# Low halves of the second feed-forward weights: from VectorE to TensorE and ScalarE, in a reordered opening

## The reference

```python
h = relu(layernorm(x))                       # block 0, a graph attention
Wh = h @ W;  e = leaky(Wh@a1 [:,None] + Wh@a2 [None,:])   # slope 0.2
att = softmax(where(adj > 0, e, -inf))
att = where(att < 16th largest of its row, 0, att)
x = x + elu(att @ Wh)
y = relu(layernorm(x))                       # block 1, three layers
for l in range(3):
    s = leaky(y@w_i[l] [:,None] + y@w_j[l] [None,:] + b[l])
    agg = softmax(where(adj + eye > 0, s, -inf)) @ y
    z = layernorm(y + agg) * g1[l] + beta1[l]
    ff = gelu(z @ W1[l] + b1[l]) @ W2[l] + b2[l]   # 256 -> 1024 -> 256
    y = layernorm(z + ff) * g2[l] + beta2[l]
out = x + y
```

## Time and profile before

| | us |
|---|---|
| median of 3 runs | 2819.51 (2818.25 to 2822.01) |
| the profiled execution | 2820.53 |
| its span in the profile | 2818.1 |
| PE busy in the span | 2712.6 (96%) |
| ACT busy | 2328.5 (83%) |
| DVE busy | 2302.2 (82%) |
| POOL busy | 2082.3 (74%) |

### The profile page before, as it was taken

One profiled execution on the slowest core, in us unless ns is written; L12 is line 12 of the kernel. 1 busy time (PEld: TensorE's weight loads), 2 busy tenths in 40 slices (PEclk: granted clock), 3 DMA queues, 4 the chain that ended last, 5 costly groups with the idle time before them and its releaser, 6 DMA issues.

```text
span 2818.1 us, 55394 instructions
## 1 busy us (share of the span) xinstructions
PE 2712.6 (96%) x17764; PEld 2441.1 (87%) x17764; DVE 2302.2 (82%) x7766; ACT 2328.5 (83%) x4808; POOL 2082.3 (74%) x2217
## 2 busy tenths in 40 slices
PE   5799999999999999999999999999999999999995
PEld 4688888889899999889999899999989998888884
DVE  6889878888888888888888888888888888887542
ACT  3788898888888888888888888888888888888763
POOL 1466777787777778877778777777877777877774
PEclk9899999999999999999999999999999999999997
DMA  5110110101110110110110111011111011010001
GB/s 167 47 29 22 36 31 28 35 9 35 34 35 27 35 25 19 35 35 28 35 35 9 35 35 35 27 35 22 22 35 35 28 36 33 14 22 20 11 10 15
DMA packets 96323, 88.64 MB, mean 31 GB/s; under 512 B 9120, under 2 KB 94368, under 8 KB 96032
## 3 DMA queue, kind: packets, MB, share of 16 engines
q1 hardware_dynamic: 79136, 68.32, 7.9%
q0 software_dynamic: 16896, 16.78, 4.6%
HBM read 47.34 MB, written 37.75 MB: 30 GB/s over the span
## 4 chain that ended last, share of the span: by engine, by line
PE 72%; POOL 9%; issue 7%; ACT 6%; DVE 4%; DMA 2%; SPq 0%; POOLq 0%; ACTq 0%; DVEq 0%
PE ps_ff L3065 10%; PE ps_mm L3042 10%; PE ps_mm L3044 9%; PE ps_ff L3066 9%; PE ps_ff L3067 9%; PE ps_mm L3043 9%; PE ps_ag L3100 5%; PE ps_ht L3112 2%; POOL a_lo L506 2%; PE ps L3164 2%; DMA out<-H 2%; POOL H L496 1%; PE ps_s L3088 1%; POOL H L513 1%; ACT X L1083 1%
## 5 line engine op out<-in xcount | busy, mean ns | idle before, releaser
L3065 PE MATMUL ps_ff<-w_hi,a_hi 128*128 128x256 f32 x3072 | 892.9, 291 | 12.6 <-POOL a_lo L506 5.9
L506 POOL TENSOR_TENSOR a_lo<-A,a_hi 128x512 fp32r<-128x512 f32 x384 | 527.3, 1373 | 482.6 <-ACT a_hi L1077 482.3
L3066 PE MATMUL ps_ff<-w_lo,a_hi 128*128 128x256 f32 x3072 | 855.2, 278 | 0.0
L3067 PE MATMUL ps_ff<-w_hi,a_lo 128*128 128x256 f32 x3072 | 854.6, 278 | 0.0
L1069 ACT ACTIVATE A<-ps_mm,b_col 128x512 f32<-128x512 f32 x768 | 517.3, 685 | 250.3 <-PE ps_ff L3067 140.7
L3042 PE MATMUL ps_mm<-ht_hi,w_hi 128*128 128x512 f32 x1536 | 625.7, 407 | 6.7 <-DVE ht_lo L2327 4.3
L3065 PEld LDWEIGHTS ps_ff<-w_hi,a_hi 128*128 128x128 f32 x3072 | 577.9, 188 | 50.6 <-issue 13.3
L3044 PE MATMUL ps_mm<-ht_lo,w_hi 128*128 128x512 f32 x1536 | 605.5, 394 | 0.0
L3043 PE MATMUL ps_mm<-ht_hi,w_lo 128*128 128x512 f32 x1536 | 603.6, 393 | 0.0
L3066 PEld LDWEIGHTS ps_ff<-w_lo,a_hi 128*128 128x128 f32 x3072 | 579.0, 188 | 12.1
L3067 PEld LDWEIGHTS ps_ff<-w_hi,a_lo 128*128 128x128 f32 x3072 | 579.0, 188 | 0.0
(11 more groups left out here) (120 smaller groups left out, 5320.8 us busy)
## 6 DMA issues: line engine op xcount, KB each, us to landing
xr<-in_x SPq DMA_DIRECT2D x32, 512.0 KB, 4.0
out<-x SPq DMA_DIRECT2D x32, 512.0 KB, 4.8
out<-H POOLq DMA_DIRECT2D x32, 512.0 KB, 6.1
mask_in<-mask_park SPq DMA_DIRECT2D x96, 128.0 KB, 4.0
adj_sb<-in_adj SPq DMA_DIRECT2D x32, 256.0 KB, 4.4
mask_park<-mask_out SPq DMA_DIRECT2D x32, 128.0 KB, 3.9
X<-in_L_gnn_W SPq DMA_DIRECT2D x3, 1024.0 KB, 5.2
H<-in_L_gnn_W SPq DMA_DIRECT2D x3, 1024.0 KB, 8.6
```

What stands on the lines that cost most here:

```text
L506: pool.tensor_tensor(a_lo[:, at], A[:, at], a_hi[:, at].bitcast(F32), ALU.subtract).then_inc(s["a_lo_gpsimd"], 1)
L3065: pe.matmul(out_g, a_hi[:, at, cols], w2_hi[:, l, m], start=first, stop=False, skip_group_check=True)
L3066: pe.matmul(out_g, a_hi[:, at, cols], w2_lo[:, l, m], start=False, stop=False, skip_group_check=True)
L3067: last = pe.matmul(out_g, a_lo[:, at, cols], w2_hi[:, l, m], start=False, stop=final, skip_group_check=True)
```

## The change

The low halves of W2 are made by other engines. PE writes the F32 staging values through the identity into a bank, and subtracts the high half through a negated identity; ScalarE copies the bank out as F32R. Each layer is cut into four quarters q of 512 columns. The negated identity lies in a part of ht_hi that is free until unit (1,0). The banks are ps_ag and ps_ht for layer 0, ps_s and ps_ag for layers 1 and 2, so waits come with it that keep these apart from scores and agg.

```diff
+        neg_ident = ht_hi[:, 0, 0, 0:P]
+        def w2_bank(l, q):
+            return (ps_ag, ps_ht)[q % 2] if l == 0 else (ps_s, ps_ag)[q % 2]
...
             def load_w2(l):
-                    sp.wait_ge(s["w2_split"], l)
+                    sp.wait_ge(s["w2_split"], 4 * l)
...
             def ht_high(k, l, d):
+                if peeled(k, 1) and l == 0:
+                    act.wait_ge(s["w2_diffed"], 4 * L)
...
+            def neg_ident_copy():
+                act.wait_ge(s["const_made"], 4)
+                act.activation(neg_ident, ident[:], ACT.Copy, scale=-1.0).then_inc(s["neg_made"], 1)
+
+            def w2_low(l, q):
+                act.wait_ge(s["w2_diffed"], 4 * l + q + 1)
+                act.activation(w2_flat[2][l][:, q * 512:(q + 1) * 512], w2_bank(l, q)[:], ACT.Copy).then_inc(s["w2_split"], 1)
...
-            def w2_low(l):
-                dve.wait_ge(s["w2_hi_made"], l + 1)
-                tt(w2_lo[:, l], w2_stage, w2_hi[:, l].bitcast(F32), ALU.subtract).then_inc(s["w2_split"], 1)
...
             def mm2(k, l, m):
-                        pe.wait_ge(s["w2_split"], l + 1)
+                        pe.wait_ge(s["w2_split"], 4 * l + 4)
             def turn_sj(k, l):
+                if peeled(k, 1) and l == 0:
+                    pe.wait_ge(s["w2_split"], 4 * L)
             def agg(k, l, half):
+                if peeled(k, 0) and l == 0 and half == 0:
+                    pe.wait_ge(s["w2_split"], 4)
...
+            def w2_diff(l, q):
+                c, cols = 4 * l + q, slice(q * 512, (q + 1) * 512)
+                pe.wait_ge(s["w2_hi_made"], l + 1)
+                if c == 0:
+                    pe.wait_ge(s["neg_made"], 1)
+                if c > 1:
+                    pe.wait_ge(s["w2_split"], c - 1)
+                if c == 4:
+                    pe.wait_ge(s["pt_made"], 1)
+                if c == 5:
+                    pe.wait_ge(s["y1_made"], 2)
+                pe.matmul(w2_bank(l, q)[:], ident[:], w2_flat[0][:, cols], start=True, stop=False)
+                last = pe.matmul(w2_bank(l, q)[:], neg_ident, w2_flat[1][l][:, cols], start=False, stop=True)
+                last.then_inc(s["w2_diffed"], 1)
```

More of the change, by code:

```diff
@@ L1228, in opening @@
                 mix_high(1, 0)
-                w2_high(1)
+                w2_low(1, 0)
+                w2_low(1, 1)
                 h_norm(0, 0)
+                elu_exp(1, 0)
+                mix_high(1, 1)
                 ht_high(0, 0, 0)
-                mix_high(1, 1)
-                elu_exp(1, 0)
+                w2_low(1, 2)
+                w2_low(1, 3)
+                w1_high(2)
                 ht_high(0, 0, 1)
@@ L1463, in opening @@
+                h_norm(4, 0)
                 mix_high(5, 0)
-                a_high(1, 2, 3)
                 gelu(1, 2, 4)
-                h_norm(4, 0)
-                leaky(3, 1)
+                a_high(1, 2, 4)
                 ht_high(4, 0, 0)
-                a_high(1, 2, 4)
-                y_norm(2, 1)
                 gelu(1, 2, 5)
+                a_high(1, 2, 5)
                 gelu(1, 2, 6)
-                a_high(1, 2, 5)
-                exps(3, 1)
-                elu_exp(5, 0)
+                gelu(1, 2, 7)
@@ L1476, in opening @@
                 a_high(1, 2, 6)
                 ht_high(4, 0, 1)
-                p_copy(3, 1)
-                mix_high(5, 1)
-                gelu(1, 2, 7)
-                gelu(4, 0, 0)
-                a_high(1, 2, 7)
-                elu_exp(5, 1)
-                a_high(4, 0, 0)
-                gelu(4, 0, 1)
+                a_high(1, 2, 7)
+                y_norm(2, 1)
+                mix_high(5, 1)
+                leaky(3, 1)
+                gelu(4, 0, 0)
+                elu_exp(5, 0)
@@ L1497, in opening @@
-                leaky(2, 2)
-                ht_high(3, 1, 0)
-                gelu(4, 0, 6)
-                a_high(4, 0, 6)
-                gelu(4, 0, 7)
-                ht_high(3, 1, 1)
-                a_high(4, 0, 7)
-                r_norm(5)
+                a_high(4, 0, 3)
+                elu_exp(5, 1)
+                gelu(4, 0, 4)
+                gelu(4, 0, 5)
+                a_high(4, 0, 4)
+                h_norm(3, 1)
+                gelu(4, 0, 6)
+                a_high(4, 0, 5)
@@ L3196, in opening @@
                 agg(0, 0, 0)
+                w2_diff(1, 0)
+                agg(0, 0, 1)
                 turn_z(1)
-                agg(0, 0, 1)
                 z_mix(1, 0)
+                w2_diff(1, 1)
+                z_agg(1, 0)
+                w2_diff(1, 2)
+                z_mix(1, 1)
+                w2_diff(1, 3)
+                turn_h(0, 0, 0)
                 w1_bias(2)
-                z_agg(1, 0)
-                turn_h(0, 0, 0)
-                z_mix(1, 1)
                 turn_h(0, 0, 1)
@@ L3215, in opening @@
                 mm1(0, 0, 6)
+                w2_diff(2, 0)
+                w2_diff(2, 1)
+                mm1(0, 0, 7)
                 mm2(0, 0, 3)
-                mm1(0, 0, 7)
+                w2_diff(2, 2)
+                w2_diff(2, 3)
                 mm2(0, 0, 4)
+                turn_sj(1, 0)
                 mm2(0, 0, 5)
```

1016 lines of the change are left out of this document (515 added, 501 removed).

## The result

The changed kernel takes 2829.31 us, the median of 6 runs (2828.93 to 2831.16); the kernel before took 2820.29 beside it. The ratio is 1.0031, with a 95% interval of 1.0021 to 1.0041: 9 us slower, where 3 us faster was forecast, and outside the range. The profiled execution has a span of 2827.1 us against 2818.1.

The account below looks back on a forecast made before the run. TensorE, busy 96%, was taken to bound the kernel after a serial opening chain; -1.3 us to mm1(0,0,0), -1.7 to mm1(1,0,0) and 0 after gave -3.0 us, a median of 2816.5, 8 in 10 within 2810.5 to 2823.5.

Parts of the forecast that it names:

- (J): Everything after mm1(1,0,0): no change, 0, with bounds of -7.6 and +3 us.
- (A): Start of the kernel: load_a0 second in SP's queue shortens VectorE's wait of 2.59 us; -1.0 us.
- (B): Layer 0 differences in TensorE's waits around z_mix and z_agg; +0.8, 0 and +0.9 us at the upper clock.
- (C): In group 0's attention, z_out(0,1) no longer waits behind other VectorE work that now comes later; -2.8 us.
- (D): Differences fill TensorE's waits, so the clock rises from about 31 us and z_agg and z_mix shorten; -3.6 us.
- Rival 1: Slower: TensorE stays at the lower clock until mm1(0,0,0); +7.4 us, 2826.9 us, chance 0.10.
- (E): From r_moments(0) to node_scores(0,0), VectorE's work there of 7.1 us exceeds the 6.2 us latency; +0.9 us.
- (G): w2_diff(1,0) between the two halves of agg, in a wait of 1.1 us; +0.6 us.
- (H): From agg(0,0,1) to mm1(0,0,0), three more differences and w1_bias(2) moved later; +2.9 us, bounds +2.0 and +6.3.
- (I): Unit (0,0) and the way to mm1(1,0,0), ScalarE's list setting the pace; -1.7 us, bounds -4 and +1.5.
- Rival 3: Clearly faster: the new opening order also saves about half the 7.6 us idle after 160 us; -8.1 us, chance 0.25.
- Rival 2: No change: unit (0,0) pays +1.5 us as differences push mm1 and mm2 back; total +0.2 us, chance 0.17.

Follow-up runs that it names:

- the first seam: Changed kernel up to mm1(1,0,0), about 135 us, on every engine, then the order of the kernel before; 2815.65 us, 0.9981 of the kernel before.
- the seam at 272: Changed kernel's queues up to mm1(0,2,6), at 272 us, then the order of the kernel before; its total time is not given in the text.
- the seam at 345: Changed kernel's queues up to mm1(1,2,3), at 345 us, then the order of the kernel before; as slow as the changed kernel.
- the two kernels with moved steps: Changed kernel with add_out(1) behind a_low(3,1,6) on GpSimd, 2829.37 us (1.0029); the same plus ht_low(3,1,1) ahead of y_sum(4,0) on VectorE, 2830.93 us (1.0034).

## Why the prediction was wrong

The step that failed is **(J)**, everything after mm1(1,0,0): 0, with bounds of -7.6 and +3. It measured +9.5 us to the end of the span: +12.4 by the end of the opening, and some -3 in the closing, which no step of the prediction had. I took the idle time of before as what there was to gain, and an order that waits "somewhat more" as all there was to lose, though the five queues were rewritten up to 500 us, and no row of before can bound what a different order waits. The new order without the differences loses 12.9 us there, the differences in the old order nothing; and the kernel with the seam at 135, which has the changed kernel up to mm1(1,0,0) and the old order behind it, is 0.19% faster than before. That it is 5.7 us faster and not 0.5 is no merit of the forecast: most of it arises outside the opening.

The other steps:

- **(A)** -1.0: DVE starts on the row sums at 8.38 in place of 9.27, -0.9. Right. W0 now lands last, its bound.
- **(B)** A difference takes 2.24 us at the lower level (28.27 to 30.51) and 1.09 at the upper (34.40 to 35.49), against 2.3 and 1.15; the twelve copies take 0.58 to 0.60 each by their groups in the trace. Right. With **(C)** and **(D)**, z_out(0,1) starts 6.1 us earlier, forecast -5.7. The clock rises at 31 us, as forecast, and the two orders, each with and without the differences, show that these bring it. Rival 1 is refuted.
- **(E)** +0.9: from r_moments(0), 6.1 us early, to node_scores(0,0), 5.4 early: +0.7. Right. **(F)** 0: agg(0,0,0) starts 5.5 early. Right.
- **(G)** +0.6: agg(0,0,1) starts 4.7 early, so +0.8. Right, at its lower level.
- **(H)** +2.9, bounds +2.0 to +6.3: from there to mm1(0,0,0) it is +5.3. The work was counted rightly; 0.8 of the error is agg(0,0,1) itself at 1.2 GHz (1.91 us in place of 1.10), and 1.3 z_agg(1,1) at 1.2 GHz, from 78.8 us, behind w1_bias(2). My bound had w1_bias(2) itself at the lower level; it took 3.63 us as before, and the lower level came behind it.
- **(I)** -1.7: -1.1. ACT waited 0.57 and 1.91 us for the two last pairs of differences (2.1 forecast), but a_high(0,0,7) ends at 107.6, not at 105, and leaky(1,0) is 0.7 us early in place of 3.4; y1_sum(1,0,0) keeps 0.3 of it.

So at mm1(1,0,0) the sum was -0.5 where -3.0 was forecast: right in the mechanism, 2.5 us too hopeful, nearly all of it in (H). The mark for a wrong prediction, mm1(0,0,0) at 84 or later, stayed silent at 81.74. The mark that "would show (J)", PE's idle time of 7 to 8 us from 160 to 500 us, measured 13.9. Rival 3 had the place of the surprise right and its sign wrong: it asked whether the new order saves idle time there and never what happens if it makes some. Rival 2 put four differences in unit (0,0) at +1.5, and that unit did not pay it.

## What to carry to other kernels

A rewritten order of in-order queues is a change of its own, and it can't be priced by the idle time it finds: look at the diff stretch by stretch for steps of one chain that move back against the matmuls, and allow for a whole chain coming late wherever one engine's queue has ready work put ahead of it. Where a change has a new piece of work and a new order, put the old order back from a point where both have done the same steps; here that kept the work, cost nothing at the first seam and took the loss away. In a stretch where TensorE is nearly full, a wait of 1.4 us can cost 3, and need not: count the time at the lower clock behind it, and don't expect it back by moving the step that was waited for, if the rest of its chain is as late.

## What the hardware showed

In the changed kernel the granted clock went to 0.50 for 3.4 us at 188.0, 399.6 and 426.9 us, behind waits of 1.42 and 0.47, of 1.40, and of 2.44 us in an otherwise full stretch; in the kernel before it went down at 193.7 us behind two waits close together, of 0.89 and 1.07 us, that ended at 191.13 and 193.29. The length of the wait doesn't decide it: the clock stayed at 1.00 behind a wait of 1.41 us at 452.98 in the kernel before, of 1.85 us at 284.22 with the seam at 272, and of 1.42 and 0.63 us at 186.93 and 188.21 with the seam at 345, where PE takes the same steps as in the changed kernel, as it did behind single waits of 0.96 and 1.18 us in the two kernels with moved steps. The wait at 284.22 us, and PE's busy time behind it (seam at 272):

```profile
284.22 0.38 PE L3086 MATMUL ps_ff<-w_hi,a_hi 128*128 128x256 f32 x1 [1.85 <-DVE a_lo L2360]
...
284.00:288.00 4.00, 3.78 (x33) 3.78 (x34) 3.63 (x12) 0.00 (x0) 1.87 (x4) 1.00 0.00 0
```

The Trainium skill, "TensorE: Matmul & The Clock Gate", HAM oscillation, names longer gaps in its rule for the fall; the falls in these rows disagree, and they decide. The section behind it, A second HAM failure mode, tells of short idle times that do the same when they come often, which is nearer to these rows.

The 32 products of one column of w1_bias(2), 3.63 us without a gap at 74.07, didn't hold the clock up: it is low right behind them, from 78.8 us, in the changed kernel, as from 74.3 behind the same products in the kernel before.

An instruction of DVE with two inputs from SBUF waited out GpSimd's instruction to its very end, twice: 2.73 and 1.47 us in place of 0.35, ending 0.16 and 0.15 us behind GpSimd's a_low. The Trainium skill, "SBUF — State Buffer", Who interferes with whom, tells of an exclusive lock between the two engines, and these rows agree; in the first case GpSimd's DMA issue stood ahead of a_low and DVE waited through both.
